# Deep-interest recommender on one core: one softmax per tile, and its weighted rows added in the next tile

## The reference, cut to what matters

```python
mask = seq_inputs[:, :, 0] != 0
other_info = concatenate([dense_inputs] + [emb_sparse[i][sparse_inputs[:, i]] for i in range(3)])
seq_embed = concatenate([emb_seq[i][seq_inputs[:, :, i]] for i in range(2)])      # (2048, 40, 128)
item_embed = concatenate([emb_seq[i][item_inputs[:, i]] for i in range(2)])       # (2048, 128)
q = broadcast_to(item_embed[:, None, :], seq_embed.shape)
info = concatenate([q, seq_embed, q - seq_embed, q * seq_embed])
h = sigmoid(info @ att_W1 + att_b1)          # 80 wide
h = sigmoid(h @ att_W2 + att_b2)             # 40 wide
logits = where(mask, (h @ att_Wf + att_bf)[..., 0], NEG_INF)
att = softmax(logits, axis=-1)               # over the 40 steps
user_info = einsum('bl,bld->bd', att, seq_embed)
info_all = concatenate([user_info, item_embed, other_info])
info_all = bn_gamma * (info_all - bn_mean) * rsqrt(bn_var + BN_EPS) + bn_beta
info_all = prelu(info_all @ ffn_W1 + ffn_b1, ffn_a1)
info_all = prelu(info_all @ ffn_W2 + ffn_b2, ffn_a2)
return sigmoid(info_all @ out_W + out_b)
```

## Time and profile before

| | |
|---|---|
| median of 3 runs | 1684.45 us (1682.66 to 1688.41) |
| profiled execution, its own time | 1686.11 us |
| its span, first to last instruction | 1684.1 us |
| mean granted TensorE clock | 0.945 of full |
| TensorE busy | 1441.7 us, 86% |
| GpSimd busy | 1207.2 us, 72% |
| VectorE busy | 887.8 us, 53% |
| ScalarE busy | 472.9 us, 28% |

### The profile page before, as it was taken

One profiled execution on the slowest core, in us unless ns is written; L12 is line 12 of the kernel. 1 busy time (PEld: TensorE's weight loads), 2 busy tenths in 40 slices (PEclk: granted clock), 3 DMA queues, 4 the chain that ended last, 5 costly groups with the idle time before them and its releaser, 6 DMA issues.

```text
span 1684.1 us, 23703 instructions
## 1 busy us (share of the span) xinstructions
PE 1441.7 (86%) x7687; PEld 795.0 (47%) x7687; DVE 887.8 (53%) x2246; ACT 472.9 (28%) x823; POOL 1207.2 (72%) x1269
## 2 busy tenths in 40 slices
PE   0599897989889897998979797998979899798988
PEld 0355453545445454554535454454545455354542
DVE  6636555464644636464543746355464735446453
ACT  3323232232313222241322323132332313222233
POOL 6777777777777777777777777777777767777710
PEclk9999998999989998999989999999989999999995
DMA  7411111111111111111111111111111111111200
GB/s 158 100 26 46 27 46 28 27 46 27 46 27 46 26 27 47 27 45 27 46 28 27 46 27 46 27 46 27 33 41 27 46 25 46 27 34 39 27 7 0
DMA packets 59538, 64.27 MB, mean 38 GB/s; under 512 B 33477, under 2 KB 33811, under 8 KB 59407
## 3 DMA queue, kind: packets, MB, share of 16 engines
q0 software_dynamic: 40448, 41.50, 12.3%
q1 hardware_dynamic: 16898, 12.98, 2.9%
q10 hardware_dynamic: 2062, 8.08, 1.8%
HBM read 62.36 MB, written 0.11 MB: 37 GB/s over the span
## 4 chain that ended last, share of the span: by engine, by line
PE 76%; DVE 11%; issue 7%; ACT 4%; DVEq 1%; ACTq 1%; DMA 0%
PE grown L410 45%; PE pre L447 9%; PE pre L449 8%; PE mid L456 5%; PE mid L463 3%; DVE sums L962 3%; DVE pool L799 3%; PE turned L430 2%; PE mid L398 1%; PE turned L435 1%; DVE picked L911 1%; DVE split L792 1%; ACT L656 1%; DVE hist L787 1%; ACT hist_t L651 1%
## 5 line engine op out<-in xcount | busy, mean ns | idle before, releaser
L340 POOL DMA_INDIRECT hist<-in_L_rec_emb_seq_dram,idx x1184 | 1131.2, 955 | 360.9 <-issue 329.2
L410 PE MATMUL grown<-pool,split 128*128 128x384 bf16 x4782 | 888.8, 337 | 138.6 <-DVE pool L799 136.8
L410 PEld LDWEIGHTS grown<-pool,split 128*128 128x128 bf16 x4782 | 463.8, 101 | 551.4 <-issue 181.9
L799 DVE TENSOR_SCALAR pool<-rel 128x768 bf16<-128x768 bf16 x797 | 390.0, 542 | 0.0
L895 DVE TENSOR_TENSOR prod_t<-turned,item_t 128x512 f32<-128x512 f32 x160 | 109.0, 688 | 379.6 <-ACT hist_t L651 379.6
L656 ACT ACTIVATE hidden<-pre 80x512 f32<-80x512 f32 x160 | 94.8, 593 | 541.2 <-DVE pre L903 540.9
L903 DVE TENSOR_TENSOR pre<-pre,item_part 80x512 f32<-80x512 f32 x160 | 111.1, 695 | 215.4 <-PE pre L449 215.4
L447 PE MATMUL pre<-hist_t,w_hist 128*80 128x512 f32 x320 | 174.1, 627 | 0.0
L449 PE MATMUL pre<-prod_t,w_raw 128*80 128x512 f32 x320 | 164.3, 595 | 0.0
L962 DVE SCALAR_TENSOR_TENSOR sums<-hist,weight,sums 128x128 f32<-128x128 f32 x576 | 159.9, 347 | 0.0
L661 ACT ACTIVATE pool<-mid,b 128x256 f32<-128x256 f32 x160 | 76.0, 475 | 202.2 <-PE mid L456 202.2
(11 more groups left out here) (124 smaller groups left out, 592.6 us busy)
## 6 DMA issues: line engine op xcount, KB each, us to landing
hist<-in_L_rec_emb_seq_dram,idx POOLq DMA_INDIRECT x1184, 2.4
keys<-key_rows SPq DMA_DIRECT2D x30, 384.0 KB
hist<-in_L_rec_emb_seq_dram ACTq DMA_DIRECT2D x6, 672.0 KB
keys<-key_rows ACTq DMA_DIRECT2D x4, 384.0 KB
hist<-in_L_rec_emb_seq_dram ACTq DMA_DIRECT2D x2, 728.0 KB
sparse_rows<-in_L_rec_emb_sparse_dram,idx_sparse POOLq DMA_INDIRECT x48, 3.3
raw<-in_r_seq_inputs_dram SPq DMA_DIRECT2D x1, 600.0 KB, 4.6
hist<-in_L_rec_emb_seq_dram ACTq DMA_DIRECT2D x6, 90.0 KB
```

Source lines behind the costliest of these rows:

```text
L340: gp.indirect_dma_start(rows, None, table, bass.IndirectOffsetOnAxis(ap=index, axis=0)).then_inc(landed, 16)
L410: last = nc.tensor.matmul(grown[n][:, 0:MC], split[n][:, c, k, :], hot[:, slot, n * MC:(n + 1) * MC], start=(c == 0 and k == 0), stop=(c = ...
L799: last = nc.vector.tensor_scalar(hot[:, slot, :], rel[half][:, :, 0:RC], float(c), None, ALU.is_equal)
```

## The change

The early softmax is gone. A tile has one softmax over its 40 logits after its last group. The weights are computed by ScalarE in step 0 of the next tile (`weigh`), and VectorE adds the 40 weighted rows in steps 0 to 3 of the next tile, 2, 3, 3 and 2 groups (`ROWS_AT`), then the user row. TensorE turns the user row in step 4 and does its three products in step 5, in the PSUM bank of the sums instead of that of layer 2. The first softmax operation and the last logits now stand after all chunks of a tile; sixteen instead of thirteen chunks of the next tile are made hot before its start, of which thirteen are used. The first pair of tiles is written out ahead of the loops, which run over the other seven. The numbers for the sparse gathers are computed in tile 0 and not before it.

`hist` of a tile is in use for longer. GpSimd's wait for a free half is therefore in two stages: its first gather waits until 5 groups of the tile before are added (`PACE`), and its gather of group 5 until the user row is made.

```diff
@@ GpSimd
                     wait(gp, idx_ready, tile + 1)
-                    wait(gp, tile_consumed, tile + 2)
+                    wait(gp, sum_step, tile * L + PACE * G)
...
+                        if g == PACE:
+                            wait(gp, user_ready, tile + 1)
@@ TensorE, a tile's steps
-                    for g in range(EARLY):
...
-                        if g == 0:
-                            pe.wait_ge(item_part_ready, tile + 1)
-                            finish(tile + 1, 1 - half)
...
+                for g in range(GROUPS):
+                    if g < SHARE:
+                        at, to, other = AHEAD + g * PER, tile, half
+                        ends = [at + 2, at + 4, CH if g == SHARE - 1 else at + PER]
+                    elif g > SHARE:
+                        at, to, other = (g - SHARE - 1) * PER, tile + 1, 1 - half
+                        ends = [at + 2, at + 4, at + PER]
+                    else:
+                        at, to, other, ends = 0, tile, half, [0, 0, 0]
+                    if g < LAST:
+                        turn_group(g + 1)
+                    grow(to, other, at, ends[0])
+                    layer1(g)
+                    grow(to, other, ends[0], ends[1])
+                    if g >= 2:
+                        logits_of(g - 2)
+                    if g == 0:
+                        pe.wait_ge(item_part_ready, tile + 1)
+                    if g >= 1:
+                        layer2(g - 1)
+                    if not first and g == len(ROWS_AT):
+                        turn_user(tile - 1)
+                    if not first and g == len(ROWS_AT) + 1:
+                        part_of(tile - 1, 1 - half)
+                    grow(to, other, ends[1], ends[2])
+                turn_rows()
+                logits_of(LAST - 1)
+                layer2(LAST)
+                grow(tile + 1, 1 - half, 2 * PER, AHEAD)
+                logits_of(LAST).then_inc(logits_done, 1)
@@ ScalarE
+            def weigh(tile):
+                act.preload_act_table(ACT.Exp)
+                act.wait_ge(max_ready, tile + 1)
+                nc.scalar.activation(weight[:, :], logit[:, :], ACT.Exp, bias=neg_max[:, :], accum_out=total[:, :])\
+                    .then_inc(weights_ready, 1)
+                act.preload_act_table(ACT.Sigmoid)
...
+                for g in range(GROUPS):
+                    if g >= 2:
+                        sigmoid2(g - 2)
+                    if g < LAST:
+                        copy_group(g + 1, (g + 1) % 2)
+                    if not first and g == 0:
+                        weigh(tile - 1)
+                    sigmoid1(g, g % 2)
...
+                act.wait_ge(rows_turned, tile + 1)
+                nc.scalar.copy(hist[:, half, SD * D:L * D], turned[0][:, 0:MC]).then_inc(rows_copied, 1)
+                sigmoid2(LAST - 1)
+                sigmoid2(LAST)
@@ VectorE
+            def add_rows(tile, half, step):
+                if step == 0:
+                    wait(dve, weights_ready, tile + 1)
+                    nc.vector.reciprocal(inv_total[:, :], total[:, :])
+                for g in ROWS_AT[step]:
+                    if g == LAST:
+                        dve.wait_ge(rows_copied, tile + 1)
+                    add_group(tile, half, g)
+                if step == len(ROWS_AT) - 1:
+                    user_row(tile)
...
+                    if g < LAST:
+                        product(g + 1, (g + 1) % 2)
+                    if g == SHARE:
+                        pick()
+                        dve.wait_ge(rel_ready, tile + 2)
+                    heat(to, other, first_hot, ends[0])
+                    if g == 0:
+                        wait(dve, item_part_ready, tile + 1)
+                    add_item(g, g % 2)
+                    heat(to, other, ends[0], ends[1])
+                    if not first and g < len(ROWS_AT):
+                        add_rows(tile - 1, 1 - half, g)
```

More of the change, by code:

```diff
@@ L48, in build @@
     W = 2 * P
-    EARLY = 7
+    SHARE = 7
+    ROWS_AT = ((0, 1), (2, 3, 4), (5, 6, 7), (8, 9))
+    PACE = 5
     UP = 64
@@ L63, in build @@
     AHEAD = 13
+    MADE = 16
     RANGES = [(0, 13), (13, 25), (25, 37), (37, 49)]
@@ L377, in _ @@
         def _(pe):
-            pe.sem_inc(tile_consumed, 2)
             pe.wait_ge(ident_ready, 16)
@@ L389, in _, with turn_user, part_of @@
             pe.wait_ge(keys_copied, 1)
-            def finish(done, half):
-                pe.wait_ge(user_ready, done)
-                nc.tensor.transpose(mid[:, 3 * P:4 * P], user[:, :], ident[:, :]).then_inc(user_turned, 1)
-                pe.wait_ge(user_copied, done)
-                pe.sem_inc(tile_consumed, 1)
+            def turn_user(tile):
+                pe.wait_ge(user_ready, tile + 3)
+                nc.tensor.transpose(sums[:, 2 * P:3 * P], user[:, :], ident[:, :]).then_inc(user_turned, 1)
+            def part_of(tile, half):
+                pe.wait_ge(user_copied, tile + 1)
                 for c in (1, 2, 0):
                     k = CHUNKS[c][1]
-                    last = nc.tensor.matmul(mid[0:H1, 0:P], fw1[0:k, c, :], x[half][0:k, c, :], start=(c == 1), stop=(c == 0))
+                    last = nc.tensor.matmul(sums[0:H1, 3 * P:4 * P], fw1[0:k, c, :], x[half][0:k, c, :], start=(c == 1),
+                                            stop=(c == 0))
                 last.then_inc(part_done, 1)
@@ L526, in turn_sparse @@
+            for half in range(2):
+                body(half, half, 0, half == 0)
+            with pe.Fori(1, PAIRS) as pair:
+                for half in range(2):
+                    body(pair * 2 + half, half, pair, False)
+            turn_user(TILES - 1)
+            part_of(TILES - 1, 1)
+            pe.wait_ge(part_ready, TILES)
             def turn_sparse(p):
@@ L715, in _, with final_user, final_part @@
-            finish(TILES + 1, 1).then_inc(part_ready, 1)
+            def final_user(tile, half):
+                act.wait_ge(user_turned, tile + 1)
+                normalised(x[half][:, 0, :], 0, sums[:, 2 * P:3 * P]).then_inc(user_copied, 1)
+            def final_part(tile):
+                wait(act, part_done, tile + 1)
+                nc.scalar.activation(part[:, bass.ds(tile * P, P)], sums[0:H1, 3 * P:4 * P], ACT.Identity, bias=fb1[:, :])\
+                    .then_inc(part_ready, 1)
@@ L717, in copy_sparse @@
+            for half in range(2):
+                body(half, half, 0, half == 0)
+            with act.Fori(1, PAIRS) as pair:
+                for half in range(2):
+                    body(pair * 2 + half, half, pair, False)
+            weigh(TILES - 1)
+            final_user(TILES - 1, 1)
+            final_part(TILES - 1)
             def copy_sparse(p):
@@ L751, in _ @@
             nc.vector.memset(dense_rows[:, TILES, :], 0.0)
-            for h in range(2):
-                nc.vector.memset(x[h][:, :, :], 0.0)
-            nc.vector.memset(user[:, :], 0.0)
-            dve.sem_inc(softmax_step, 2)
+            dve.sem_inc(user_ready, 2)
+            dve.sem_inc(sum_step, 2 * L)
             nc.vector.memset(masked_logit[:, :], MASKED)
@@ L800, in heat @@
                     last.then_inc(hot_ready, 1)
-                if end == CH:
+                if first < end == CH:
                     dve.wait_ge(hot_ready, tile * CH + CH)
@@ new lines, in _, with add_group @@
+            nc.vector.tensor_copy(dense_now[:, 0, :], dense_rows[:, 0, :]).then_inc(dense_ready, 1)
+            def add_group(tile, half, g):
+                before = tile * L + 2 * L
+                for k in range(G):
+                    row = hist[:, half, (g * G + k) * D:(g * G + k + 1) * D]
+                    column = g * G + k // 2 + 2 * (k % 2)
+                    by = weight[:, column:column + 1]
+                    acc = odd_acc if k % 2 else even_acc
+                    if g == 0 and k < 2:
+                        nc.vector.tensor_scalar(acc, row, by, None, ALU.mult).then_inc(sum_step, 1)
+                    else:
+                        dve.wait_ge(sum_step, before + (g * G + k - 1))
+                        nc.vector.scalar_tensor_tensor(acc, row, by, acc, ALU.mult, ALU.add).then_inc(sum_step, 1)
@@ L1023, in prelu1 @@
+            heat(0, 0, AHEAD, MADE)
+            dve.wait_ge(idx_rest_loaded, 32)
+            for half in range(2):
+                body(half, half, 0, half == 0)
+            with dve.Fori(1, PAIRS) as pair:
+                for half in range(2):
+                    body(pair * 2 + half, half, pair, False)
+            for step in range(len(ROWS_AT)):
+                add_rows(TILES - 1, 1, step)
             def prelu1(p):
                 dve.wait_ge(ffn1_done, p + 1)
-                nc.vector.tensor_tensor(z1[:, :], pre1[0][0:H1, 0:W], part[:, bass.ds(p * W + P, W)], ALU.add).then_inc(z1_step, 1)
+                nc.vector.tensor_tensor(z1[:, :], pre1[0][0:H1, 0:W], part[:, bass.ds(p * W, W)], ALU.add).then_inc(z1_step, 1)
```

448 lines of the change are left out of this document (147 added, 301 removed).

## The result

The changed kernel takes 1634.04 us, median of 4 runs (1633.04 to 1634.67). The kernel before, run beside it, takes 1683.56 (1681.73 to 1688.41). The ratio is 0.9701, 95% interval 0.9679 to 0.9723: 49.5 us faster. The forecast was 1636.

A forecast was written before the change was run, and what follows sets the result against it. Before, TensorE's boundary stops behind VectorE's late work bound the kernel; after, gathers: tile 15's start 1446.8, group 7 +89.9, last logits +34.2, softmax, bare adds, user row to 1584.0, then 51.4: span 1635.4, forecast 1636 us, range 1628 to 1656.

The forecast's parts named there:

- The gathers allow 2.4 us a tile, plus their lead: GpSimd's gathers take 94.885 us a tile against TensorE's 97.3, which limits whatever the change saves on TensorE.
- The sum of TensorE's tile, 84.4 us: TensorE's work in one tile of the changed kernel, counted step by step at full clock: 84.4 us.
- The row adds at nothing: VectorE's 12 adds each in steps 1 and 2 fit, 7.0 of 8.06 us, covered by three hot chunks ready ahead.
- The graded wait at nothing: GpSimd's two-stage wait for a free half never holds the gathers; there are 45 us of room.
- Where the stall goes: The 10.5 us left per tile become TensorE waits of about 2 us before turned groups 2 to 7.
- The new waits cost nothing: TensorE's new waits of about 2 us leave the clock up, judged by a 1.86 us stop followed by full clock.
- clock rival: Short waits drop TensorE's clock, 1.5 us a burst; six fit in 10.5 us, nine a tile decide, twelve give 1749; 5%.
- No low-clock chunks at the boundary: Sign of being right: chunks at the tile boundary would not run at the low clock.
- group 7 at S + 72 x 1.2485 = S + 89.9: Group 7 of a tile is announced 89.9 us after the start S of its gathers, at the next group's seventh gather.
- The cycle is longer than the gathers': Rival: TensorE and VectorE's tile misses 84.4 by over 10.5 us; 1653 at 96.1 us a tile; 8%.
- The graded wait holds the gathers: Rival: row adds delayed beyond 45 us hold GpSimd's gathers; 1776 us at 55 us of delay; 2%.
- Gathers do not rule: Rival: gathers get quicker or landed groups are used earlier, so 84.4 us a tile gives 1498 us; 1%.

The follow-up runs named there:

- experiment 1: Last of eight gathers left out of groups 0 to 8: changed kernel 1501.06 us (0.8912), kernel before 1682.82 us (0.9998).
- experiment 3: Changed kernel with all row adds in step 0 of the next tile: 1636.83 us; with an eighth of the gathers also left out: 1633.76 us.
- experiment 2: Changed kernel with one wait, for the user row of the tile before, in place of the graded wait: 1633.04 us, ratio 0.9697.
- experiment 5: Changed kernel with the two-input subtractions that split the table in the first tile made one-input multiplications: 1626.86 us, ratio 0.9676.
- experiment 6: Changed kernel with the last tile's row adds laid over the final network of pairs 0 to 6: 1622.76 us, ratio 0.9651.
- experiment 7: Kernel with last row adds over the final network, plus unused matmuls on TensorE: 1619.56 us with 4 in each later pair, 1619.38 with 12.

## Why the prediction was right, step by step

**What bounds the kernel before** was right. Fewer gathers leave it at its time (experiment 1), fewer adds at the boundary shorten it (experiment 4).

**"The gathers allow 2.4 us a tile, plus their lead"** was right, and is what made the number. 94.88 us a tile measured, 94.885 forecast; with fewer gathers the same kernel is 133 us faster.

**The sum of TensorE's tile, 84.4 us**: 85.2 measured (experiment 1), and mostly 84.75 inside a pair. Most of the rest is at the boundaries where a pair begins. From the last logits to the first chunks it takes 4.08 us there (806.92 to 811.00) and 3.05 inside a pair (239.75 to 242.80); the terms made 3.1, logits 0.44, the 2.2 and a second turned group 0.43. The 1 us more is what the working had set apart as waits at code jumps.

**The row adds at nothing** was right as to the time. Their placement counts (8.8 us a tile in experiment 3), and spread over four steps they make no chunk late. That the three chunks ready ahead are what covers them was not tried.

**The graded wait at nothing** was right: one wait in its place gives the same time (experiment 2).

**Where the stall goes**: before the turned groups, as forecast, but groups 2 to 8 and from 0.2 to 2.2 us each, not 2 us before each of groups 2 to 7. They are 94.7 us in all, 6.8 a tile, where 94.9 - 85.2 = 9.7 are free; part of the rest goes into the stretches at the low clock. The gathers rule from tile 2 on (the first wait for them is at 257.62), not from tile 1.

**The new waits cost nothing** was right as to the time, and the reason given for it, that they leave the clock up, was not. The mean granted clock did rise, to 0.969 (0.945 before), and after most waits the clock is full, as after one of 2.16 us:

```profile
837.45 0.66 PE L423 MATMUL turned<-ident,hist 128*128 128x128 f32 x4 [2.16 <-POOLq L360]
837.94 2.12 PE L405 MATMUL grown<-pool,split 128*128 128x384 bf16 x12
```

But of the 19 waits of 1.70 us and more, seven were followed by the low level, twelve not; none of the 16 from 1.50 to 1.67 us was. So the length of the stop alone doesn't tell which. Twelve matmuls then took 3.06 to 3.79 us instead of 2.11, at most two such bursts in a tile. The working's 1.86 us row was one case of full clock, too little for "they leave it up". What saved the forecast is the condition in its own clock rival: bursts that fit into the 10.5 us left a tile are free. "No low-clock chunks at the boundary", a sign of being right, did not come either: four boundaries have them, with no effect on the end.

The Trainium skill (TensorE: Matmul & The Clock Gate, A second HAM failure mode: psum-queue depth-cycling) says that a TensorE that often idles for a moment between groups of matmuls swings between its two levels. The trace agrees in seven of 82 waits.

**The term that was mis-sized** is "group 7 at S + 72 x 1.2485 = S + 89.9". Of the last tile's groups 7 and 8 in the changed kernel:

```profile
1531.01 0.66 PE L423 MATMUL turned<-ident,hist 128*128 128x128 f32 x4 [0.74 <-POOLq L360]
...
1540.91 0.66 PE L423 MATMUL turned<-ident,hist 128*128 128x128 f32 x4 [0.66 <-DMA hist<-in_L_rec_emb_seq_dram,idx]
```

Group 7 is turned at 1531.0 = S + 83.7. The last of its gathers (number 65 of the tile, counted from zero) starts at S + 65 x 1.2485 = S + 81.2 and lands about 2.5 us later, which is S + 83.7: the signal comes when the group has landed, not when GpSimd begins gather 72, ahead of which it stands in the code. The line of the signal itself shows it, the last of its 128 at 1530.9:

```profile
L360 POOLq EVENT_SEMAPHORE  x128: 17/17/17, 29.4 to 1530.9; - x128
```

So GpSimd carries out waits and signals ahead of gathers that stand before them in its code and have not begun. Then group 8, at S + 93.6, is also turned as it lands (S + 91.1 + 2.5). From there to the last logits it is 25.5 us, as worked out (34.2 - 9.0 = 25.2). The end is 4.5 us early, 1566.4 for 1570.9.

**The rest of the sum**, forecast and measured: S of tile 15 1446.8, 1447.3; last logits to user row 13.1, 12.7 (bare adds 10.8, 10.4); from there to the end 51.4, 51.9; span 1635.4, 1631.0; profiled execution on the device 1637.4, 1633.0. So the sum was 4.4 us too high, nearly all of it group 7. That the forecast of 1636 is only 2 us off the median of 1634.0 is in part luck: it took off 1.7 us because the profiled execution before lay that far above its median, and the one after lay 1.0 below. For the "own range" of 1629 to 1648 the listed bounds give a lower end of 1632; the measured time is inside either way.

**The rivals.** *The cycle is longer than the gathers'*: no, 85.2; bunched adds bring it within about 1 us of true (93.8 and 94.5). *The clock*: it fell eleven times in the loops, never more than twice in a tile, where nine times a tile were needed. *The graded wait holds the gathers*: no. *Gathers do not rule*: no; its 1498 us is what the kernel does once an eighth of them is gone, 1501.

## What to carry to other kernels

Before you count what a faster engine brings, take the pace of the next engine over the whole span from its first to its last instruction: here GpSimd was "busy" 72% and had 2.4 us left in 97. Once such a pace rules, time saved elsewhere is worth nothing and time lost by the first item on it is paid in full at the end: look for the gain at the start (8.3 us in experiment 5) and behind the last item (11.3 us in experiment 6). A signal that stands between gathers in GpSimd's code should be costed at the landing it waits for, not at the gather that it stands before. And a mean granted clock of 0.969 doesn't say where the clock fell: look at every burst of the same matmuls, and then at whether the wait behind it had room.

## What the runs showed of the hardware that was not expected

- GpSimd's waits and signals run ahead of its gathers: the signal that stands ahead of gather 72 of a tile (counted from zero) came with the landing of gather 65, 6.2 us before gather 72 began.
- Gathers, which last 0.94 us elsewhere, lasted up to 4.02 us beside VectorE's float32 operations over 128 x 1536 elements, with two inputs and, less, with one (2.43). Beside the row adds, 40 per tile, they kept it: 94.88 us a tile, and 76 x 1.2485 is 94.89.
- A TensorE that is busy by the records can be at 1.2 GHz for a whole stage. In the changed kernel's final network:

```profile
1582.00:1631.00 49.00, 41.99 (x97) 12.78 (x96) 16.10 (x40) 15.87 (x33) 15.67 (x16) 0.50 0.13 12
```

  42 of 49 us busy, granted clock 0.50 throughout, as in the kernel before. Added matmuls of 384 columns brought it to 0.90 (experiment 7): busy time in the records did not bring the clock back; with four added matmuls a pair it came back once (1584.9) and not after 1595.8. Which property of theirs counts was not tried.
- A stop of 1.94 us with the short float32 products of the final network around it was followed by the low level to the end. Between the dense steps of a tile, stops of 1.70 to 2.24 us were followed by the low level seven times in 19, each time for some 3 us only.
